# Gate loops: one step's sums, the column sums of two older steps, the next step's sums

## The reference, cut to what matters

```python
hg = jnp.einsum('bnf,gf->bng', h3, Wg[:, :F])
qg = jnp.einsum('blf,gf->blg', q, Wg[:, F:]) + bg
attn = jax.nn.sigmoid(hg[:, :, None, :] + qg[:, None, :, :])
qi = jnp.einsum('bnlf,blf->bnf', attn, q)
```

## Time and profile before

| | before |
|---|---|
| median of 3 runs | 1166.58 us (1166.46 to 1171.52) |
| the profiled execution's own time | 1168.65 us |
| its span, first to last instruction | 1166.9 us |
| mean granted TensorE clock | 0.975 |
| PE busy | 1103.3 us (95%) |
| DVE busy | 761.0 us (65%) |
| ACT busy | 572.4 us (49%) |
| POOL busy | 180.0 us (15%) |

### The profile page before, as it was taken

One profiled execution on the slowest core, in us unless ns is written; L12 is line 12 of the kernel. 1 busy time (PEld: TensorE's weight loads), 2 busy tenths in 40 slices (PEclk: granted clock), 3 DMA queues, 4 the chain that ended last, 5 costly groups with the idle time before them and its releaser, 6 DMA issues.

```text
span 1166.9 us, 17791 instructions
## 1 busy us (share of the span) xinstructions
PE 1103.3 (95%) x7530; PEld 917.5 (79%) x7530; DVE 761.0 (65%) x1066; ACT 572.4 (49%) x603; POOL 180.0 (15%) x96
## 2 busy tenths in 40 slices
PE   7999998999999999998999789999999999999987
PEld 6889985444799954447599779867999999999984
DVE  7994755888534258885353644245888888888862
ACT  0433226888333268882242533124666666666630
POOL 2434613555000035550000000000000000000000
PEclk9999999999899999999998899799999999999998
DMA  8042285221142552112242004405877777777730
GB/s 286 11 151 95 83 279 140 74 56 38 56 177 92 198 154 73 56 37 81 81 147 99 1 1 163 158 1 178 269 245 243 245 244 246 244 245 243 247 113 28
DMA packets 82211, 162.71 MB, mean 139 GB/s; under 512 B 4050, under 2 KB 60142, under 8 KB 81838
## 3 DMA queue, kind: packets, MB, share of 16 engines
q1 hardware_dynamic: 80736, 151.86, 38.9%
q0 software_dynamic: 1392, 9.66, 3.2%
HBM read 157.86 MB, written 0.80 MB: 136 GB/s over the span
## 4 chain that ended last, share of the span: by engine, by line
PE 68%; DVE 19%; ACT 6%; issue 4%; DMA 1%; POOL 1%; SPq 0%; DVEq 0%; ACTq 0%; POOLq 0%
PE PS L963 12%; PE PS L830 7%; PE PS L712 6%; PE PS L464 6%; PE PS L626 4%; PE PS L728 4%; PE PS L451 4%; DVE Wlo L1743 3%; PE PS L602 3%; PE PS L977 3%; PE PS L946 3%; ACT Whi L1288 3%; PE PS L882 3%; PE PS L533 2%; DVE PRD L1534 2%
## 5 line engine op out<-in xcount | busy, mean ns | idle before, releaser
L1743 DVE TENSOR_TENSOR Wlo<-W,Whi 128x2304 fp32r<-128x2304 f32 x68 | 173.7, 2556 | 43.5 <-ACT Whi L1288 43.4
L1288 ACT CAST Whi<-W 128x2304 fp32r<-128x2304 f32 x68 | 144.4, 2126 | 0.1
L963 PE MATMUL PS<-Whi,Mhi 128*128 128x384 f32 x408 | 139.6, 342 | 3.4 <-DVE Mlo L1772 3.4
L963 PE MATMUL PS<-Wlo,Mhi 128*128 128x384 f32 x408 | 136.5, 335 | 0.0
L963 PE MATMUL PS<-Whi,Mlo 128*128 128x384 f32 x408 | 136.5, 335 | 0.0
L425 POOL TENSOR_TENSOR PRDP<-arena 128x1024 f32<-128x1024 f32 x48 | 114.5, 2385 | 119.9 <-PE PS L728 88.4
L712 PE MATMUL PS<-QH,SEL 128*128 128x512 f32 x384 | 116.9, 426 | 9.7 <-DVE arena L1534 3.6
L712 PEld LDWEIGHTS PS<-QH,SEL 128*128 128x128 f32 x384 | 65.5, 190 | 60.7 <-DVE PRD L1534 22.7
L1155 ACT ACTIVATE arena<-PS 128x1024 f32<-128x1024 f32 x96 | 98.4, 1025 | 27.8 <-PE PS L712 27.8
L1155 ACT ACTIVATE PS<-PS 128x1024 f32<-128x1024 f32 x96 | 98.0, 1021 | 0.0
L963 PEld LDWEIGHTS PS<-Whi,Mhi 128*128 128x128 f32 x408 | 76.7, 188 | 8.2 <-DVE Mlo L1772 8.2
(11 more groups left out here) (269 smaller groups left out, 2428.8 us busy)
## 6 DMA issues: line engine op xcount, KB each, us to landing
W<-in_L_rel SPq DMA_DIRECT2D x68, 1152.0 KB, 5.6
W<-in_W_rel SPq DMA_DIRECT2D x6, 2304.0 KB, 8.4
W<-in_W SPq DMA_DIRECT2D x6, 2304.0 KB, 8.4
arena<-in_qU SPq DMA_DIRECT2D x96, 128.0 KB, 2.6
W<-in_WqT SPq DMA_DIRECT2D x4, 2304.0 KB, 9.2
W<-in_W_root SPq DMA_DIRECT2D x2, 2304.0 KB, 13.3
W<-in_WgT SPq DMA_DIRECT2D x2, 2304.0 KB, 8.9
QH<-QH POOLq DMA_DIRECT2D x2, 1536.0 KB, 10.3
```

Source lines behind the costliest of these rows:

```text
L963: mm = pe.matmul(PS[:, 4 + s % 2, 0:HALF], MS[a][mb][:, k, j * P:(j + 1) * P], WS[b][w % 3][:, k, :], start=n == 0, stop=n == 17)
L1288: nc.scalar.copy(WS[0][w % 3][:], W[(FIRST34 + r) % 2][:, :, q * HALF:(q + 1) * HALF]).then_inc(w_hi, 1)
L1743: V.tensor_tensor(WS[1][w % 3][:], W[(FIRST34 + r) % 2][:, :, q * HALF:(q + 1) * HALF], WS[0][w % 3][:].bitcast(F32), ALU.subtract).then_i ...
```

## The change

Inside each pass of the loop, `sums(c + 1)` is moved from ahead of the two reduces to behind them. No instruction is added or taken away, and each keeps its own wait.

```diff
                 for c in range(0, STEPS + 4, 2):
                     if c < STEPS:
                         sums(c)
-                        sums(c + 1)
                     if c >= 4:
                         reduce(c - 4)
                         reduce(c - 3)
+                    if c < STEPS:
+                        sums(c + 1)
```

## The result

| | before | after |
|---|---|---|
| median of the runs compared | 1169.05 us (4 runs, 1166.46 to 1172.74) | 1184.82 us (4 runs, 1184.12 to 1187.32) |
| span of the profiled execution | 1166.9 us | 1182.4 us |
| first loop, first sums to the last unit's copy | 293.05 - 181.11 = 111.9 | 303.47 - 183.44 = 120.0 |
| second loop, the same | 526.14 - 415.44 = 110.7 | 541.65 - 423.00 = 118.7 |

The change makes the kernel slower: the ratio is 1.0129, with a 95% interval of 1.009 to 1.0168. The median before in this comparison holds one more run than the one shown ahead of the prediction, and lies 2.5 us higher.

A forecast was written before the change was run, and what follows sets the result against it. TensorE was taken to bound the loop, VectorE's products right behind. Per gate +7.5 (steps 16 to 94), +1.1 (start) and +0.3 (end) make 8.9, +18 us for both: 1184.5 us, range 1177 to 1192.

The forecast's parts named there:

- The chain: From an odd step's sums through sigmoid and VectorE's PSUM product to the even sums reusing its banks: 3.09 us.
- The cycle: Gate loops after the change: 3.09 us, even sum 0.66, two reduces 1.00; 4.75 us for four steps instead of 4.42.
- Steps 16 to 94: Steady part of each gate loop: 93.6 us against 86.14, so +7.5 us a gate.
- the unit's copy: VectorE's copy of a finished unit's sums, every 16 steps: delays the odd product by 0.2 us, five times a gate.
- The loop's start: Steps 0 to 16 of a gate: step 5's sum now stands behind two reduces; about +1.1 us, bounds 0 and 3.
- The loop's end: Last reduces of a gate: they wait for step 95's product at 4.75 us instead of GpSimd's at 4.29; +0.3 us.
- The sum: All terms over the gate loops: 8.9 us a gate, +18 us for both, giving 1184.5 us.
- No difference: Rival: the wait on the product hides in TensorE's turn-over, if the chain is below 2.65 us; +2 us, 1168.6, chance 6%.
- faster: Rival: TensorE runs at its own 2.13 us a pair, if sum to product fits 2.63; -8 us, 1158.5, chance 4%.
- The clock: Rival: new TensorE gaps lower the clock; +12 us, 1196.5, with a tenth of the loops slow, +120 with all; chance 4%.
- third rival: GpSimd's product is locked out by VectorE's even products and waits up to 1.22 us; +28 us, 1194.5, chance 3%.
- TensorE's own 17.04: Gate loops: 16 steps at TensorE's pace of 2.13 us a pair, 8 x 2.13 = 17.04, against 17.68 before.

The follow-up runs named there:

- Kernels 2: Kernel before, old order, with odd and even steps' roles swapped (even steps' sigmoids in PSUM, GpSimd takes c % 4 == 1); 1184.5 us, ratio 1.0143.
- kernel 5: Changed kernel with odd and even steps' roles swapped and the reduces one step later; 1164.33 us, ratio 0.9946 to before.
- kernel 4: Changed kernel with VectorE's product of odd steps cut from 1024 to 768 columns, part of the result left out; 1174.93 us, ratio 1.0076 to before.
- kernel 8: Kernel before with the copy of a finished unit's sums moved from behind step 9's predecessor, step 8, to behind step 9; 1168.49 us, ratio 0.999.
- kernel 6: Changed kernel with VectorE's product of odd steps cut from 1024 to 512 columns, part of the result left out; 1164.82 us, ratio 0.9958 to before.
- kernel 7: Kernel before with VectorE's product of odd steps cut from 1024 to 768 columns, part of the result left out; 1160.36 us, ratio 0.9929.
- kernel 1: Changed kernel with odd and even steps' roles swapped (even steps' sigmoids in PSUM, GpSimd takes c % 4 == 1); 1190.84 us, ratio 1.0191 to before.

## Why the prediction was right

The chain was right. That the forecast of 1184.5 us lies 0.3 from the measured 1184.82 is partly luck: the increase was forecast at 18 us and measured at 15.8, and the median before in the comparison is 2.5 higher than the one that the forecast set out from.

- **The cycle.** 3.09 + 0.66 + 1.00 = 4.75 us for four steps was forecast, and the timeline shows 3.09, 0.66, 1.00 and 4.75 to 4.76. Kernels 2 and 5 show that it is this chain and not the order, kernel 4 that VectorE's product lies on it at its full length.
- **Steps 16 to 94.** Forecast +7.5 us, measured (297.60 - 204.94) - 86.14 = +6.5. The term that was too large is the unit's copy, five times 0.2. The forecast asked how late the next odd product would be with pairs of equal length, and that came true once: before the first copy of the first loop the ways from odd to even sum are 0.74 and 0.69, the copy holds the product back from 217.93 to 218.13, and the four steps with it take 4.95 instead of 4.75 (5.09 in the second loop). From then on the split is 0.93 or more against 0.50 or less, the copy ends as the next sigmoid does, and the other four copies of each loop cost nothing.

The first copy, with step 25's sigmoid ahead of it and step 25's product behind it:

```profile
216.88 1.01 ACT L1156 ACTIVATE PS<-PS 128x1024 f32<-128x1024 f32 x1 [0.46 <-PE PS L712]
...
217.80 0.42 DVE L1522 COPY hN<-PS 128x256 f32<-128x256 f32 x1
...
218.13 1.22 DVE L1535 TENSOR_TENSOR PRD<-PS,arena 128x1024 f32<-128x1024 f32 x1
```

- **The loop's start.** Forecast +1.1. First sums to step 16: 20.37 before, 204.94 - 183.44 = 21.50 after, +1.1; the second loop showed +0.9. The granted clock was the same on both sides, 0.92 in the first loop's start and 0.91 in the second's. What it costs there shows in kernel 8, whose first loop starts with the order and the copies of before: 18.84 at a clock of 1.00 instead of 20.37.
- **The loop's end.** Forecast +0.3, measured (302.33 - 297.60) - 4.29 = +0.4. The reason given was the wrong one: step 94's sums now stand second in their pair, so its sigmoid comes later, and with it GpSimd's product. Step 95's product ended at 301.08 + 1.23 = 302.31, as late as GpSimd's, but its reduce stands behind step 94's anyway.

The start of step 16, and the last sums and reduces of the first loop after (answering to the earlier trace rows):

```profile
204.94 0.19 PEld L712 LDWEIGHTS PS<-QH,SEL 128*128 128x128 f32 x1 [0.44 <-DVE PRD L1535]
...
297.60 0.30 PEld L712 LDWEIGHTS PS<-QH,SEL 128*128 128x128 f32 x2 [0.17 <-DVE arena L1535]
...
302.33 0.16 PEld L728 LDWEIGHTS PS<-PRDP,selmem 128*32 128x32 f32 x8 [1.81 <-POOL PRDP L425]
```

- **The sum.** The two loops grew by 8.1 and 8.0 us, 16.0 in all, against the 18 forecast. The spans differ by 15.5. The rest is outside the loops: the first loop starts 2.3 us later (183.44 against 181.11), and the way from one loop to the next is 2.9 shorter. The latter is the clock: in the windows of the 11 us behind the first loop it was granted 0.69 before and 1.00 after.

Before:

```profile
293.00:304.00 11.00, 9.59 (x36) 8.12 (x37) 7.72 (x9) 4.52 (x5) 0.00 (x0) 0.69 0.00 0
```

After:

```profile
303.00:314.00 11.00, 9.57 (x56) 8.06 (x49) 8.32 (x10) 4.96 (x7) 0.00 (x0) 1.00 0.00 0
```

I do not put this down to the change: kernel 6 has the changed order and from its first loop's last reduce load to its second loop's first sums load it takes 123.05 us, as in the kernel before; kernel 7 has the old order and takes 120.19, as the changed kernel does. Of the other profiles only kernel 8's has 123.05. What made the first loop start later I did not find.

- **The rivals.** "No difference" and "faster" needed the chain to fit into 2.63 us; it is 3.09. The clock stayed at full in the steady part, 1.00 from 194 to 299 and from 433 to 537 us. GpSimd was not locked out: its products last 2.38 us on average. But GpSimd did decide in kernel 1, by its plain length, which neither the prediction's rivals nor that run's expectation held.

## What to carry to other kernels

In a loop where engines pass steps around a ring of buffers, write down for each buffer who frees it, and add up the chain from its fill to its next fill; then see how much of the loop the order puts between the two. Moving one block in the order changes which step has the short way. Where two kinds of steps take turns, the kind with the longer chain should be filled last in its group, and a slow engine's step needs its reduce a group later; the kernel before and kernel 5 have both. Kernel 5 is the fastest version here that does all the work, 0.5% under the kernel before. In the steady parts that is 2.6 us, as much as kernel 8 gained (2.7), and in both the copy stands ahead of a GpSimd step, where VectorE has room (in kernel 5 it runs from 231.93, and the next product starts at 232.70 after a wait of 0.35 for its sigmoid). That this is kernel 5's gain is argued from the rows; no run took it apart, and the other 3.7 us of the 0.5% lie outside the steady parts.

## What the runs showed of the hardware

VectorE's products with both inputs in SBUF took longer the more they overlapped with a GpSimd product, once the overlap was more than about 0.15 us. Before, the median of the 24 `PRD<-arena` ones was 1.29 us and the longest 1.39. In the changed kernel, where none begins more than 0.15 us before a GpSimd product ends, these 24 took 1.215 to 1.235:

```profile
L1535 DVE TENSOR_TENSOR PRD<-arena x24: 1215/1216/1235, 191.2 to 530.9; 128x1024 f32<-128x1024 f32 x24
```

In kernel 5 they begin up to 0.38 us before its end, and reach 1.46 us:

```profile
240.62 2.40 POOL L425 TENSOR_TENSOR PRDP<-arena 128x1024 f32<-128x1024 f32 x1 [2.14 <-PE PS L728]
...
242.64 1.46 DVE L1535 TENSOR_TENSOR PRD<-arena 128x1024 f32<-128x1024 f32 x1
...
245.28 0.76 PEld L712 LDWEIGHTS PS<-QH,SEL 128*128 128x128 f32 x4 [0.63 <-DVE PRD L1535]
```

The product began 0.38 us before GpSimd's ended (243.02) and took 0.24 longer. The PSUM product behind it was late for it, and the sums at 245.28 waited 0.22 more than the usual 0.41. GpSimd's own 2.4 us do not change.

This agrees in kind with what the Trainium skill says in SBUF — State Buffer, section "Who interferes with whom": the one that comes second waits for the first. In size the lengthening was less than the overlap: 0.06, 0.17 and 0.24 us for overlaps of 0.20, 0.31 and 0.38, and next to nothing up to 0.15. In all ten traces VectorE came second; no GpSimd product began under a VectorE product of two SBUF inputs, so the third rival's mechanism is not shown by any run.

By these rows the longer product accounts for most of what is left between kernel 5's 17.45 and TensorE's own 17.04 a unit, two waits of 0.22. That is argued and not tested: no run took it away.
